# Attention sum of a graph network: the weighing product in four pieces, and 49 count lists dealt 9, 30, 10 over three blocks

## What is computed

```python
# layer 0: i = src, j = dst; four heads of 64 columns
out_j = softplus(concat(h[j], edge_attr) @ W).reshape(-1, 4, 64)
alpha = segment_softmax(softplus(batchnorm(...)), i)      # one weight per edge and head
msg   = out_j * alpha[:, :, None]                         # the weighing product
aggr  = segment_sum(msg, i, 6250)
x     = x + aggr.mean(1) + bias
# layer 1: sum of the neighbours' rows
x     = x + segment_sum(h[src], dst, 6250)
```

## Time and profile before

| what | value |
|---|---|
| runs | 16427.04, 16422.82, 16393.09 us; median 16422.82 |
| profiled execution | 16422.03 us, span 16420.4 us |
| busy over the span | PE 43%, PEld 31%, DVE 45%, ACT 28%, POOL 65% |
| POOL, the six slices from 7389 to 9852 us | 8, 8, 8, 8, 7, 7 tenths |
| DVE, the same slices | 6, 6, 6, 6, 1, 0 tenths |
| POOL L1118, count scatters | 1568 in 2065.4 us, mean 1317 ns |

### The profile page before, as it was taken

How to read it: one execution, slowest core, us unless ns; L and a number is a source line. 1 busy time by engine, 2 the same in 40 slices (tenths; PEclk the granted TensorE clock), 3 DMA queues, 4 the chain that set the end, 5 groups by cost and what they waited for, 6 DMA issues and landing times. The chain is left out here.

```text
span 16420.4 us, 145244 instructions
## 1 busy us (share of the span) xinstructions
PE 7024.2 (43%) x27706; PEld 5057.3 (31%) x27706; DVE 7327.3 (45%) x13292; ACT 4660.4 (28%) x8183; POOL 10717.1 (65%) x9774
## 2 busy tenths in 40 slices
PE   2344444444444444410555006863333463333377
PEld 1233333333333333310555002223333323333233
DVE  9566666666666566656666100122222222222311
ACT  5455454555444444411666000010000010000010
POOL 7677777777777777738888772027777527777600
PEclk9777677777777777655566558855555555555578
DMA  0444444444443344371666105521111121111146
GB/s 14 111 129 126 132 126 132 126 132 124 124 125 124 122 124 124 120 49 31 183 182 182 26 5 207 208 75 25 26 26 25 41 83 26 26 26 26 22 172 216
DMA packets 867747, 1600.94 MB, mean 97 GB/s; under 512 B 510485, under 2 KB 518653, under 8 KB 817264
## 3 DMA queue, kind: packets, MB, share of 16 engines
q1 hardware_dynamic: 536176, 1173.07, 23.3%
q0 software_dynamic: 331392, 426.19, 11.1%
HBM read 1091.51 MB, written 505.30 MB: 97 GB/s over the span
## 5 line engine op out<-in xcount | busy, mean ns | idle before, releaser
L1397 POOL DMA_INDIRECT l2s_got<-rel_d,l2s_idx x3232 | 3211.4, 994 | 2337.1 <-POOLq L1394 1433.5
L1423 PE MATMUL l2s_ps<-l2s_got,l2s_oh 128*128 128x65 f32 (+1 forms) x6464 | 1473.5, 421 | 2757.5 <-PEq L1421 2757.5
L1118 POOL DMA_INDIRECT count_d<-all_list_val,all_list_idx x1568 | 2065.4, 1317 | 503.1 <-issue 463.1
L1423 PEld LDWEIGHTS l2s_ps<-l2s_got,l2s_oh 128*128 128x128 f32 x6464 | 1409.2, 331 | 2824.6 <-issue 2824.6
L642 POOL DMA_INDIRECT edge_gath<-h_d,edge_idx_s x1576 | 1712.4, 1087 | 618.3 <-issue 430.8
L646 POOL DMA_INDIRECT edge_gath<-h_d,edge_idx_d x1576 | 1694.4, 1075 | 480.3 <-issue 479.0
L654 POOL DMA_INDIRECT rows_d<-edge_rows,edge_place x1576 | 1642.5, 1042 | 480.1 <-issue 463.6
L788 DVE SCALAR_TENSOR_TENSOR edge_rows<-edge_z,edge_soft 128x1024 f32<-128x1024 f32 x784 | 952.5, 1215 | 2194.9 <-DVEq L786 2194.4
L1100 DVE TENSOR_TENSOR net_acc<-net_acc,l2s_ps 128x65 f32 (+1 forms) x3232 | 720.3, 223 | 2699.6 <-DVEq L1445 1704.0
L721 PE MATMUL edge_z<-edge_w_i,edge_in_i 128*128 128x256 f32 x3140 | 1324.6, 511 | 724.0 <-PEq L750 411.3
L714 PE MATMUL edge_tp<-all_ident,edge_gath 128*128 128x128 f32 x1576 | 428.5, 428 | 2170.2 <-DMA edge_gath<-h_d,edge_idx_d 1887.1
(11 more groups left out here) (342 smaller groups left out, 12668.4 us busy)
## 6 DMA issues: line engine op xcount, KB each, us to landing
at_rows<-rows_d SPq DMA_DIRECT2D x444, 528.0 KB
count_d<-edge_zero SPq DMA_DIRECT2D x196, 1024.0 KB
edge_srow<-in_src SPq DMA_DIRECT2D x197, 512.0 KB, 4.9
edge_lrow<-lo_d SPq DMA_DIRECT2D x197, 512.0 KB, 6.2
l1s_cnt<-count_d SPq DMA_DIRECT2D x49, 1600.0 KB, 6.7
l3s_cnt<-count_d SPq DMA_DIRECT2D x49, 1600.0 KB, 6.5
rel_d<-l2t_out SPq DMA_DIRECT2D x100, 768.0 KB, 3.2
l1s_cnt<-count_d SPq DMA_DIRECT2D x49, 1536.0 KB, 6.4
```

What stands on the lines that cost most here:

```text
L1118: pool.indirect_dma_start(out=cells, out_offset=bass.IndirectOffsetOnAxis(ap=net.list_idx[i][:, k:k + 1], axis=0), in_=net.list_val[i][:, ...
L1397: pool.indirect_dma_start(out=got[r][:, j, 0:cols], out_offset=None, in_=table, in_offset=bass.IndirectOffsetOnAxis(ap=idx[i][:, k:k + 1], ...
L1423: ins = pe.matmul(ps[q][:, j, 0:wide], oh[q][:, j, :], got[r][:, j, 0:wide], start=True, stop=True)
```

## The change

The two numbers that deal the lists are changed, and the weighing product of a group is issued as four instructions of two tiles (512 numbers per partition) each, with no wait between them. The fourth signals `weighted`, for which DVE waits ahead of L1251.

```diff
-LISTS_SOFTMAX, LISTS_ATTENTION = 6, 35
+LISTS_SOFTMAX, LISTS_ATTENTION = 9, 30
@@ attention_sum, prepare
                     rq = rows[r][:, :, :, :].rearrange("p g t r -> p (g t) r")
-                    v.tensor_tensor(
-                        wtd[q][:, :, :].rearrange("p g (h d) -> p g h d", h=HEADS),
-                        rq[:, :, 0:OUTJ].rearrange("p g (h d) -> p g h d", h=HEADS),
-                        wts[r][:, :, :, :].rearrange("p g t h -> p (g t) h").unsqueeze(3)
-                        .to_broadcast([P, G, HEADS, D]), ALU.mult).then_inc(weighted, 1)
+                    wq = wts[r][:, :, :, :].rearrange("p g t h -> p (g t) h").unsqueeze(3)
+                    for n in range(0, G, 2):
+                        ins = v.tensor_tensor(
+                            wtd[q][:, n:n + 2, :].rearrange("p g (h d) -> p g h d", h=HEADS),
+                            rq[:, n:n + 2, 0:OUTJ].rearrange("p g (h d) -> p g h d", h=HEADS),
+                            wq[:, n:n + 2, :, :].to_broadcast([P, 2, HEADS, D]), ALU.mult)
+                    ins.then_inc(weighted, 1)
                     v.wait_ge(weighted, 1).then_inc(weighted, -1)
```

## The result

| | before | changed |
|---|---|---|
| median of four runs, same chip | 16424.93 us | 16208.11 us |
| the runs | 16393.09 to 16451.6 | 16174.52 to 16245.28 |
| profiled execution | 16422.03, span 16420.4 | 16215.34, span 16213.8 |

The ratio is 0.9869, with a 95% interval of 0.9841 to 0.9898: 1.3% faster. The forecast was 16181 us, a ratio of 0.9853. First the chip of the forecast.

A forecast was written before the change was run, and what follows sets the result against it. POOL's chain of 49 scatter lists bounds the three blocks. Attention's POOL part: 1872.6 - 206.5 (dealing, cancelled by +124 and +82.6 elsewhere) - 1425 gives 241 us; 16422 - 241 = 16181 us, range 16102 to 16256, upper end stretched to 16280.

The forecast's parts named there:

- (a) dealing: Lists dealt 9, 30, 10 over softmax, attention and last block: net zero while POOL is last in all three.
- growth of the loop: DVE's attention loop: four pieces add 0.26 us a group, mostly within waits for rows; 0 to 57 us, taken as 10.
- (c) product holds POOL up: Attention loop: scatters wait for product pieces 0.6 us a group, the middle of 0.24 (first scatter only) and 0.94.
- message add, per group: Attention loop: the message add holds scatters up by 0.2 us a group, which with the product's 0.6 makes 0.8.
- a piece that loses to a scatter: Attention loop: a scatter that gets in first costs DVE's product piece 0.06 us, not the scatter's length.
- POOL's attention part: Attention block: 30 lists of 41.3 us plus 186 us of hold-ups make 1425 us, in place of 1872.6.
- behind 9975 only the start moves: After the three blocks, from the dense sum on: work starts earlier but takes as long, so the whole gain remains.
- The opening: Between adjacent product pieces the port is free for under 0.1 us, and a scatter already waiting takes it.
- Held through: Rival: DVE keeps the port over all four pieces in the attention loop; kernel 16450 us; 7 in 100.
- not the product: Rival: attention scatters are slow for another reason, such as row fetches, so pieces change nothing; 16422 us; 2 in 100.
- DVE pays: Rival: each scatter slipping in delays the next piece 0.83 us; two per product 16414 us, 2 in 100; three 16597, 4.
- the floor: Attention can't end before its DVE loop, 1346 us, so the change can gain at most 320 us.

The follow-up runs named there:

- e8: The changed kernel with an iota of 128 x 350 on POOL and a wait for it behind every attention scatter, chip C: 19201 us, 1.0397 of the kernel before.
- e2: The kernel before with only the lists dealt 9, 30, 10 and the product left whole, chip B: 18456 us, ratio 0.9984.

## Why the prediction was right, step by step, and where it was not

On the chip it was made for it came out at 16208, 27 us above the forecast and inside its own range. By its steps:

| step | predicted | measured |
|---|---|---|
| (a) dealing | 0 | ratio 0.9984, 30 us (B); part 206.0 shorter |
| a piece; four of them | 0.70; 2.55 us | 0.684; 2.51 us |
| start of a piece before the end of the one ahead | 0.08 us | 0.08 us (0.601 between starts) |
| growth of the loop | 10 us | 6 us (1328.9 to 1334.9) |
| (c) product holds POOL up, per group | 0.6 us | 0.41 us (91 us in 221) |
| message add, per group | 0.2 us | 0.34 us (74 us in 221) |
| a piece that loses to a scatter | +0.06 us | at most 746 ns for 684 |
| POOL's attention part | 1425 us | 1419.5 us |
| POOL's end in softmax, attention; DVE's; dense sum | 7859, 9295; 9226; 9734 | 7862, 9291; 9224; 9730 |
| behind 9975 only the start moves | 0 | 38 us given back |

*The opening.* The step that carried the sum, that a waiting scatter gets the port between two pieces, held: of 899 scatters in the loop none takes over 1.77 us, where 2.89 stood in the earlier trace rows. 248 are held up by the product, and 192 of them end 0.78 to 0.88 us behind the end of its first or second piece, with the next piece already running. "Held through" and "not the product" would have left scatters of 2 us and more. "DVE pays" would have shown pieces of up to 1.5 us; the longest takes 0.746. The rule of the Trainium skill that whoever comes first gets the pair for the whole instruction (SBUF — State Buffer, SBUF: two separate sides) is again borne out on one side alone: POOL waits for the piece to its end, a piece waits 0.06 us for a scatter.

*Two terms mis-sized, in opposite directions.* Of the 166 us over 0.957 that the scatters take, 91 fall on the product and 74 on the message add (put down by which DVE instruction ended 0.74 to 0.90 us before a late scatter). The product's 0.6 was the middle of 0.24 and 0.94; if the 0.24 of the first scatter is right, which no run shows by itself, the other 0.17 of a possible 0.70 says that three in four of the later scatters met an opening. The message add's 0.2 was carried over from before, and that was the mistake: it had been so small because the whole product set the phase. POOL was released at its end, so that the next scatter came late in the message add. Pieces let go of POOL earlier and it meets the add anywhere. That reading is argued; the 0.34 is measured. The traces agree that the add's price moves with the phase: it is 0.19 a group before (42 us in 221), as carried over, and 0.63 in e8 (138 us, chip C), where the pauses put the scatters at other moments of the group. The sum, 0.75 for 0.8, came out by these errors cancelling.

*The step that failed* is the last one, "behind 9975 only the start moves". 38 of 245 us went in gathers that were 11 ns longer each. I had no row that would have shown it, and a difference of this size lies inside the spread of the runs.

*What the prediction did not see* is that on other chips the end of the chain passes to another engine. It said that DVE last in attention would make the gain stop at the floor, and worked the point of that out (79 us of growth), but looked for growth only in DVE's own work. The growth came from the engine that was relieved: a quicker POOL issues its DMAs closer together. In the trace of before on the first chip nothing shows that this can cost anything.

## What to carry to other kernels

When an engine with a long stream of DMAs is held up by another engine's second SBUF operand, cut that operand's instruction into adjacent pieces or put one operand in PSUM: the first costs DVE 0.22 us a group here and leaves POOL 1.14 us a scatter for 1.55; the second, run on chip C alone, leaves a scatter that meets DVE 0.96 where the pieces leave it 1.24 there, and costs DVE a copy of 0.19 us a group besides. Then ask what the quicker stream does to the others, and time the kernel on several chips before believing a gain of 1%: the changed kernel was 1.3% faster than the one before on one chip and 4.2% slower on another. Where a term is carried over from the trace of before, ask which neighbour had set its phase.

## What the hardware showed that I had not expected

- Chips differ in the untouched kernel: 16425 us on one, 18486, 18489 and 18759 on three others. Between the profile of before on the first chip and e2's on B, whose code is the same there, the edge stage (first gather to last row scatter) is 1429 us longer and the two gather sums 637, together 2066 of the 2074 us between the spans. POOL's own instructions in the edge stage take no longer (4907 us for 5049); it waits. In e2, 349 long steps lie in the edge stage and 2060 behind the start of the dense sum, in before none. That they are what makes these stages slower is not shown.
- On those three some steps of the SP and DVE queues grow from 30 or 45 ns to 0.7 us while POOL issues indirect DMAs. The loop is some 1330 us long where they are 1.9 us or more apart and 2450 where they are 1.39 apart, with groups of 42 us for 6.0 (B and C); with a pause behind each fourth it is 1402 (D).
- POOL's wait for an `iota` of its own ahead of the next indirect DMA costs some 0.8 us, more than the `iota` of 8 columns (0.15 us).
- DVE's products fit 1.04 ns an element and some 150 ns fixed from 256 to 2048 elements, when they follow each other without a wait.
